# Expert-layer gathers in pieces of two that wait for the tiles, sums moved on by three tiles, a fifth stream gathered beside the tiles

## What is computed

```python
x = x + attn_a(layernorm(x), ...)   # 4 layers of 16-head attention (alibi, causal) and a 512-wide FFN
x = x + ffn(layernorm(x), ...)      # 8 experts, two for each row
x = x + attn_b(layernorm(x), ...)   # 16-head attention with rope
x = x + ffn(layernorm(x), ...)      # the same experts again
```

```python
h = gelu(einsum('bnd,edf->bnef', x, W1) + b1)
y = einsum('bnef,efd->bned', h, W2) + b2
out = einsum('bne,bned->bnd', comb, y)
```

## Time and profile before

| what | value |
|---|---|
| median of 3 runs | 2834.51 us (2833.81 to 2839.74) |
| the profiled execution's own time | 2838.04 us |
| its span in the profile | 2836.3 us |
| mean granted TensorE clock | 0.948 of full speed |
| busy: TensorE, VectorE, ScalarE, GpSimd | 2449.8, 1864.4, 1467.7, 911.5 us |

### The profile page before, as it was taken

How to read it: one execution, slowest core, us unless ns; L and a number is a source line. 1 busy time by engine, 2 the same in 40 slices (tenths; PEclk the granted TensorE clock), 3 DMA queues, 4 the chain that set the end, 5 groups by cost and what they waited for, 6 DMA issues and landing times.

```text
span 2836.3 us, 52348 instructions
## 1 busy us (share of the span) xinstructions
PE 2449.8 (86%) x19582; PEld 1526.6 (54%) x19582; DVE 1864.4 (66%) x5205; ACT 1467.7 (52%) x2646; POOL 911.5 (32%) x1038
## 2 busy tenths in 40 slices
PE   3799999999999999999999998896878888879964
PEld 2355555554555555545555554586754444547854
DVE  6877777777777777777778885332567777753112
ACT  0356666666666666666665655433234444454421
POOL 6233233333332333333323433231412332322144
PEclk9799999999999999999999999998989899999987
DMA  4252233233323332332312220456721221105754
GB/s 108 74 156 92 96 99 117 79 101 107 95 94 99 95 121 79 99 110 86 98 59 63 80 67 15 132 161 174 212 81 55 67 65 59 59 13 171 211 162 117
DMA packets 158013, 285.56 MB, mean 101 GB/s; under 512 B 22264, under 2 KB 111992, under 8 KB 156024
## 3 DMA queue, kind: packets, MB, share of 16 engines
q1 hardware_dynamic: 149376, 264.23, 30.7%
q0 software_dynamic: 8384, 17.97, 2.1%
HBM read 227.33 MB, written 95.96 MB: 114 GB/s over the span
## 4 chain that ended last, share of the span: by engine, by line
PE 52%; DVE 22%; ACT 12%; issue 5%; POOL 4%; another core or an unknown queue 3%; SPq 1%; DMA 1%; POOLq 0%; ACTq 0%; DVEq 0%
PE bank L589 9%; DVE mx L1215 8%; PE bank L551 7%; PE bank L567 6%; ACT big L816 4%; PE bank L725 4%; PE bank L661 4%; PE bank L735 4%; PE bank L650 4%; PE bank L553 2%; PE bank L517 2%; PE bank L609 2%; POOL big L1509 1%; ACT fhT L847 1%
## 5 line engine op out<-in xcount | busy, mean ns | idle before, releaser
L816 ACT ACTIVATE big<-bank 128x512 f32<-128x512 f32 x1600 | 932.1, 599 | 890.2 <-PE bank L567 496.8
L1215 DVE TENSOR_REDUCE mx<-bank 128x4 f32<-128x512 f32 x1600 | 1049.3, 685 | 421.3 <-PE bank L553 406.4
L551 PE MATMUL bank<-KS,QS 96*128 96x512 bf16 (+3 forms) x2560 | 694.9, 312 | 101.8 <-DVE mx L1215 67.0
L567 PE MATMUL bank<-QS,KS 99*128 99x512 bf16 (+3 forms) x2560 | 629.3, 308 | 34.4 <-ACT big L816 23.7
L1509 POOL TENSOR_SCALAR_AFFINE_SELECT big<-big 128x768 f32<-128x768 f32 (+1 forms) x416 | 265.3, 661 | 770.7 <-ACT big L816 770.7
L553 PE MATMUL bank<-mask_a,ident_b 128*128 128x128 bf16 x2560 | 496.3, 225 | 0.0
L551 PEld LDWEIGHTS bank<-KS,QS 96*128 96x128 bf16 x2560 | 257.4, 101 | 414.4 <-DVE mx L1215 210.6
L589 PE MATMUL bank<-big,V 128*9 128x512 f32 (+3 forms) x5120 | 434.2, 444 | 16.6 <-POOL big L1509 10.8
L567 PEld LDWEIGHTS bank<-QS,KS 99*128 99x128 bf16 x2560 | 215.5, 100 | 165.6 <-ACT big L816 82.6
L884 ACT ACTIVATE big<-bank,big 128x256 f32<-128x256 f32 x368 | 150.8, 471 | 277.7 <-PE bank L725 195.3
L553 PEld LDWEIGHTS bank<-mask_a,ident_b 128*128 128x128 bf16 x2560 | 258.8, 101 | 55.7 <-issue 32.0
(11 more groups left out here) (216 smaller groups left out, 2917.2 us busy)
## 6 DMA issues: line engine op xcount, KB each, us to landing
big<-e_pack SPq DMA_DIRECT2D x92, 578.0 KB
QS<-part_scr SPq DMA_DIRECT2D x480, 96.0 KB
KS<-part_scr SPq DMA_DIRECT2D x480, 96.0 KB
part_scr<-parts SPq DMA_DIRECT2D x80, 384.0 KB
x_rows<-in_alibi SPq DMA_DIRECT2D x47, 384.0 KB, 4.9
y_rows<-in_alibi SPq DMA_DIRECT2D x47, 384.0 KB, 5.5
big<-x_rows SPq DMA_DIRECT2D x92, 128.0 KB
y_rows<-big SPq DMA_DIRECT2D x92, 128.0 KB
```

Source lines behind the costliest of these rows:

```text
L551: mm(bk[:, col:col + w], Q[0:ROW_MAX, hh, t * P:(t + 1) * P], K[0:ROW_MAX, hh, 0:w], start=True, stop=False)
L567: last = mm(bk[:, col:col + w], K[0:ROWS, hh, t * P:(t + 1) * P], Q[0:ROWS, hh, t * P:T], start=(n == 0 or b + j < CLEARED), stop=(b + j < ...
L816: A(dst, src, ACT.Exp).then_inc(exp_done, 1)
L1215: v.tensor_reduce(dst, src, axis=AX.X, op=ALU.max).then_inc(a_used, 1)
```

## The change

In round 1 only:

- `COMBINE_FROM` goes from 7 to 12. VectorE combines streams 8, 9, 10, 11 at q = 12, 18, 24, 30, no longer at 7, 13, 19, 25. On VectorE that is three bias adds further on, and the fourth comes after the last tile.
- GpSimd's gathers of streams 8 to 12 come at the half tiles of the table `GATHER_BESIDE`, one call (two DMAs) at each of q = 1, 2, 4, 5 and six further on for the next stream. Ahead of each call stands a new wait on `ey_added`: 46 tiles of round 0, plus 31, plus max(q // 2 - 1, 0). In words: the call at q waits for the bias add of tile 30 + max(q // 2 - 1, 0). For the five streams these tiles are 30, 30, 31, 31; 32, 33, 34, 34; 35, 36, 37, 37; 38, 39, 40, 40; 41, 42, 43, 43.
- The gathers after the last tile are those of streams 13, 14 and 15. Before, the list had streams 12 to 15 there.

Round 0 gathers and combines as before. The diff:

```diff
--- before.py
+++ after.py
@@ -418,7 +418,8 @@
             return GROUPS * (S // JOBS) + (S % JOBS >= STREAMS[S // JOBS][0])
 
         ROUTE = ENC - JOBS
-        COMBINE_FROM, COMBINE_EVERY, COMBINE_BESIDE = (7, 7), (6, 6), (1, 4)
+        COMBINE_FROM, COMBINE_EVERY, COMBINE_BESIDE = (7, 12), (6, 6), (1, 4)
+        GATHER_BESIDE = {1 + 6 * S + at: (S, k) for S in range(5) for k, at in enumerate((0, 1, 3, 4))}
         COMBINE = {1: (-2, 27), 2: (-1, 8), 3: (-1, 28), 4: (1, 15), 5: (2, 15), 6: (3, 15), 7: (4, 15)}
         GATHER = {1: (-2, 15, 1), 2: (-2, 36, 1), 3: (-1, 16, 1), 4: (0, 16, 5), 5: (1, 18, 5), 6: (2, 18, 5), 7: (3, 18, 5)}
 
@@ -1551,14 +1552,16 @@
                     pool.wait_ge(x_added, 2 * ENC)
                     for i in range(2):
                         g.dma_start(QS[i][ROW_ALIBI:ROW_ALIBI + N_ALIBI, :, :], alibi[2]).then_inc(alibi_cleared, 16)
-                S, at = divmod(q - COMBINE_FROM[round_], COMBINE_EVERY[round_])
-                if q == 0 or at == 0 and 0 <= S < COMBINE_BESIDE[round_] - 1:
+                if round_ == 0 and q == 0:
                     for k in range(TT):
-                        gather(round_ * JOBS + max(S + 1, 0), k)
+                        gather(0, k)
                 if round_ == 0 and q == COMBINE_FROM[0]:
                     rsqrt(ln_index(ENC, 0))
+                if round_ == 1 and q in GATHER_BESIDE:
+                    pool.wait_ge(ey_added, ETILES + FIRST[1] + max(q // 2 - 1, 0))
+                    gather(JOBS + GATHER_BESIDE[q][0], GATHER_BESIDE[q][1])
                 if round_ == 1 and q == 2 * (ETILES - FIRST[1]):
-                    for S in range(JOBS + COMBINE_BESIDE[1], 2 * JOBS):
+                    for S in range(JOBS + 5, 2 * JOBS):
                         for k in range(TT):
                             gather(S, k)
```

## The result

| | before | after |
|---|---|---|
| median of 8 runs each, side by side | 2835.98 us (2829.6 to 2839.74) | 2824.32 us (2818.07 to 2826.83) |
| profiled execution, own time | 2838.04 us | 2818.07 us |
| its span | 2836.3 us | 2816.3 us |
| mean granted TensorE clock | 0.948 | 0.952 |

The ratio is 0.9956 (95% interval 0.9944 to 0.9967): 0.44% faster, 11.7 us between the medians. In the profiled executions the spans differ by 20.0 us; 7.3 us of that is there already before the change acts (`up` of tile 35 starts at 2712.71, against 2720.05 before; when before was run again it started at 2712.59, so this is no doing of the change), so the changed stretch itself is worth 12.7 us.

A forecast was written before the change was run, and what follows sets the result against it. TensorE bounds the last round's expert tiles, with holes where runs of GpSimd gathers stop ScalarE and VectorE. Tiles -16.2 and tail +10.0 give -6.2 us from the 2834.5 median: 2828.3 us, range 2819 to 2841.

The forecast's parts named there:

- rival A: Gathers from 2717.78 stop at 12, VectorE being caught before bias add 34: -11.2, 2823.3 us; chance 0.15.
- Nothing before 2717.78 moves: Before the last round's first gather: round 0 keeps its list, and the new waits cost GpSimd nothing themselves.
- The first run: Back-to-back gathers from 2717.78: 16 instead of 24, so the hole in the tiles shrinks from 27.4 to 17.4 us.
- Calls 9 to 12: Stream 10's gathers, each call waiting for its bias add, come in short runs with gaps: 0 us lost, up to 2.
- Calls 13 to 16: Stream 11's gathers beside the tiles close up into one run of 8: 7.0 us lost.
- The fifth stream: Stream 12's gathers, 8 in a row near tile 45, delay VectorE: 0.9 us lost, up to 7.6.
- The tail: After the last tile: 24 gathers in a row where there were 16, +10.0 us.
- -16.2: Tiles of the last round: 25.3 us lost instead of 41.5, before the added gathers at the end.
- B: Gain just eaten: 18 gathers from 2717.78, costlier later runs beside the tiles, 2838.4 us, within 0.2%; chance 0.18.
- C: Gaps of one or two microseconds between gathers don't free the engines: +13.3, 2847.8 us, slower; chance 0.15.
- D: Holes come from gathers and tile loads sharing DMA engines; pacing alone ends them: -31.5, 2803.0 us; chance 0.04.

The follow-up runs named there:

- the sums alone: Kernel before with the last round's sums moved later as in the change, without the new waits: 2756.54, 2751.96 and 2833.42 us (ratios 1.0000, 0.9989, 0.9991).
- the second profile: The changed kernel run again with no edit, on one chip with the kernel before: 2818.98 us, ratio 0.9961 to the kernel before.
- before again: The kernel before run again with no edit, for its profile on the same chip: 2824.95 us, ratio 0.9991 against 2826.83 us.

## Why the prediction was right, and where it was wrong

*Sign and size*: 2828.3 us was forecast, 2824.32 measured, both faster by more than 0.2%. The sum was -6.2 us; the medians say -11.7, the profiled stretch -12.7. So the sign came out, but the gain is nearly twice what was added up: the time lies in the range because rival A does, not because the forecast's own course of events took place. The terms:

*"Nothing before 2717.78 moves"*: held as far as can be told; the 7.3 us by which the profiled execution was ahead at tile 35 lie before every edit, and the medians differ by 11.7 us, near the 12.7 of the changed stretch.

*The first run, "I take 16", 17.4 us*: **this step failed**. The run was of 12 and tiles 35 to 38 lost 20.56 - 11.2 = 9.4 us. The scaling was right for 16: where such a run did come, in the sums alone, it lost 17.1 us. What failed was the choice between two rows. Calls seven and eight waited for bias add 34, which the run itself held up, so GpSimd stopped, and the hold with it. That is rival A (12 gathers, 12.4 us, 2823.3 us, 1 us from what was measured), to which I gave 0.15. For 12 gathers the scaling was 3.0 us too high (12.4 for 9.4; 2.1 too high for the 10.3 of the second profile). I let nine instructions that VectorE did 11 to 14 us into a run of before speak for "let through at 6.2 us". They don't: the sums waited for gathers to land, and bias add 33 for `down` of tile 33, which had ended at 2720.21, only 2.4 us into that run. The row that answers the question is bias add 34 of before itself, in the earlier trace rows:

```profile
2721.99 1.95 PE L735 MATMUL bank<-big 128*128 128x128 f32 x16
```

This is its `down`, which ended at 2723.94, 6.2 us into the run of before; VectorE was free from 2731.69 on, and the bias add came at 2738.48, 14.5 us late. (It is not "as late" as the GELUs at 2749.04, as the prediction has it: it came 9 us before the run's end.) Bias add 40, due 4.4 us into its run, had said the same. The Trainium skill gives the queue in front of VectorE as 8 instructions (Advanced Engine Details and Errata, Engine Queue Depths); I had drawn from it that bias add 34 would pass. In this trace it did not: bias add 33 was done at 2713.69 and nothing for the 13.29 us behind it. By the last section it was waiting for TensorE's signal all that time, so the trace says nothing about the depth of the queue itself.

*Calls 9 to 12, "0 (up to 2)"*: 3.5 us, with calls seven and eight, which the first run had left over. The pairs didn't keep apart. The held bias adds 34 and 35 came 0.7 us apart and freed three calls at once, and those of 36 and 37 the next three: two runs of 6 (from 2728.09 and 2737.41), each followed by one tile that takes 5.48 us instead of 3.735 (tiles 38 and 40, 1.75 us each).

*Calls 13 to 16, "one run of 8, 7.0 us"*: one run of 8 it was (from 2749.47), but it cost 3.8 us (42 to 43 took 5.97 us, 43 to 44 5.25). I had priced it from two runs of 8 of before, 6.5 and 7.6 us; in before again two runs of 8 cost 2.6 us (`up` of 38 to 41 in 13.78 us) and 5.7 (41 to 43 in 13.17), so the row was too narrow a base. One of these was followed by a gap of 3.77 us and an `up` of 2.95 us, its clock lowered in part; here the gaps ended at 2.1 us and the `up` behind them took 1.99 us. That tiles 38 to 45 lost 7.5 us in all, for the 7.0 named, is two errors that cancel: 3.5 too little and 3.2 too much.

*The fifth stream, "0.9 us"*: 2.0 us, by the mechanism named: the run of 8 from 2764.50 held the bias adds of tiles 44 and 45 until 2775.95.

*The tail, "+10.0"*: +10.2, 24 gathers in a row.

In sum: -16.2 became -24.9 + 2.0 = -22.9, and the tail +10.2. Of the rivals, B fell with its first run of 18, C fell (ScalarE took up work in gaps of 2.07 and 3.26 us), and D fell on the chips with the hold, where runs of 6 paced by the tiles still cost 1.75 us each in the first profile. The moved sums alone come out at nothing, 0.9991 with the hold (1.0000 and 0.9989 without): the 10 us that they add to the tail eat what their shorter first run gives.

## What to carry to other kernels

A wait that ties a producer to the progress of its victims regulates itself: when GpSimd's gathers held up the bias adds, the bias adds held up the gathers, and the longest run beside the tiles fell from 24 to 12. Price such a wait by the row of the same instruction, or of one that waits for the same engine at the same time into the disturbance; one that waits for something else says nothing. And repeat such a comparison on several chips before trusting it: what cures a disturbance costs where the disturbance isn't, 0.4 to 0.6% for the variants of this change that still had to wait there.

## What the hardware showed that was not expected

**The hold isn't always there.** The same kernel before took 2835.98, 2826.83 and 2836.80 us in three sets of runs and 2755.88, 2755.28 and 2754.19 us in three others: 71 to 83 us apart, and nothing between. The profiles of the slower sets have holds behind gathers, those of the faster have not one wait for "remote". One chip was in both groups at different times, so it is not the chip alone. TensorE's mean granted clock was 0.948 to 0.952 in the one and 0.957 to 0.960 in the other, and 1.00 in both where the tiles run without a hole, so the clock follows the holes and doesn't make them.

What makes the hold stays open. Not the transfers: the same gathers run beside the tiles with the DMA engines 0.83 busy and no hold, and with 0.18 busy and the hold. Nor the clock, nor GpSimd's pace, which is 1.25 us for a gather in both. The experiment that would replace the indirect DMAs by plain ones of the same issuing engine wasn't run.

**What is late in a hold is TensorE's signal.** An instruction that waits for another engine waits for a semaphore, a counter that the other raises when it is done, and the traces record when each changes. In the five profiles with holds 199 waits end with "remote", and in all 199 the semaphore is one that TensorE raises; where the record places its change, the waiting engine starts within 0.13 us. All 199 have three or more DMAs issued by GpSimd in the wait or the 7 us before it; a run of eight scatters does it as well as gathers (in before one starts at 2633.99, and TensorE's signals for the bias adds at 2641.21 and 2645.80 come 3.0 and 3.9 us after the end of its matmuls). In the change the last matmul of `down` 34 ends at 2716.61, its semaphore changes at 2727.38, and bias add 34 starts at 2727.40. Signals the other way come on time in mid-run: the copy of tile 36 ends at 2721.30 and `up` starts at 2721.36; in before bias add 33 ends at 2731.69 and `down` starts at 2731.84. So ScalarE and VectorE don't stop: work that waits for no signal of TensorE, as the sums of stream 8 at 2729.03, goes on. Whether the signals are late or the matmuls themselves end late isn't shown, since the profile's ends of matmuls are modelled.

**How long it holds, by the length of the run**: `up` to `up` over the run, TensorE lost 27.6 us with 24 gathers, 17.1 with 16, 9.4 with 12, 3.8, 6.5 and 7.6 with 8, and 1.75 with 6; the second profiles add 26.7 with 24, 10.3 with 12, and 2.6 and 5.7 with 8. In the first profiles that is, from 12 on, 1.3 to 1.5 us for each gather beyond six. Neither engine is always held to the end of the run: VectorE took up a bias add 14.3 us into the run of 16 and one 20.7 us into that of 24, ScalarE two GELUs 7.3 us and the copy 10.8 us into the run of 12.
